# Attention scores through one folded projection, and its neighbours' table subtractions moved

## The reference, cut to what matters

```python
b_ = conv1x1(x, w1, b1).reshape(Bb, Cc, N)
c_ = conv1x1(x, w2, b2).reshape(Bb, Cc, N)
d_ = conv1x1(x, w3, b3).reshape(Bb, Cc, N)
scores = jnp.einsum('bci,bcj->bij', c_, b_)
A = jax.nn.softmax(scores, axis=1)
attn = jnp.einsum('bcj,bkj->bck', d_, A)
```

## Time and profile before

| what | value |
|---|---|
| median of 3 runs | 163.59 us (163.04 to 163.64) |
| profiled execution, its own time | 163.81 us |
| its span, first to last instruction | 162.0 us |
| granted TensorE clock, mean | 0.973 of full speed |
| TensorE busy | 143.1 us (88%) |
| VectorE busy | 114.4 us (71%) |
| ScalarE busy | 87.2 us (54%) |
| GpSimd busy | 57.4 us (35%) |
| attention, S2 to the first convolution | 13.92 to 82.40 us |
| chain that ended last | TensorE 63%, VectorE 19%, issue 8%, ScalarE 5% |

### The profile page before, as it was taken

The page is one execution under the profiler, slowest core; times in us unless marked ns, Lnnn a source line. Parts: engine busy times, 40 slices in busy tenths (PEclk is TensorE's granted clock), DMA queues, the critical chain, the costliest instruction groups (busy, mean ns, idle before and its releaser), DMA issues.

```text
span 162.0 us, 2623 instructions
## 1 busy us (share of the span) xinstructions
PE 143.1 (88%) x948; PEld 65.8 (41%) x951; DVE 114.4 (71%) x270; ACT 87.2 (54%) x141; POOL 57.4 (35%) x109
## 2 busy tenths in 40 slices
PE   7888999999999999999999997999979996899400
PEld 2153422324221242222235763776357622388200
DVE  2186598897699977899860857795782477684891
ACT  3245545666754777558652303996192538422571
POOL 7008999999999904100000000000065000000360
PEclk9999999999999999999999999999999999999955
DMA  3496000000000000000000000001000000000007
GB/s 94 122 280 260 4 0 2 0 2 0 0 4 2 0 0 0 0 4 0 0 0 0 0 2 0 4 0 36 0 0 4 0 0 0 0 4 6 0 12 247
DMA packets 2044, 4.41 MB, mean 27 GB/s; under 512 B 240, under 2 KB 752, under 8 KB 1904
## 3 DMA queue, kind: packets, MB, share of 16 engines
q1 hardware_dynamic: 1888, 4.12, 8.0%
q10 hardware_dynamic: 144, 0.13, 0.3%
HBM read 3.06 MB, written 1.05 MB: 25 GB/s over the span
## 4 chain that ended last, share of the span: by engine, by line
PE 63%; DVE 19%; issue 8%; ACT 5%; DMA 3%; DVEq 0%; ACTq 0%
PE ps L395 13%; PE ps L441 12%; PE ps L384 12%; PE ps L458 6%; PE ps L455 4%; DVE nmax L969 4%; DMA wbc<-wa 3%; PE ps L603 2%; DVE dz L859 2%; DVE box_t L1169 2%; PE ps L358 2%; PE ps L347 2%; PE ps L612 2%; DVE tmpo L1080 1%; PE ps L348 1%
## 5 line engine op out<-in xcount | busy, mean ns | idle before, releaser
L649 ACT ACTIVATE probs<-ps,nmax 128x1024 f32<-128x1024 f32 x32 | 35.6, 1113 | 27.7 <-DVE nmax L969 27.1
L969 DVE TENSOR_REDUCE nmax<-ps 128x1 f32<-128x1024 f32 x32 | 39.1, 1221 | 7.2 <-PE ps L384 7.0
L395 PE MATMUL ps<-probs,dz 128*64 128x512 f32 x128 | 33.4, 616 | 1.0 <-DVE dz L859 0.6
L384 PE MATMUL ps<-c,b 64*128 64x512 f32 x128 | 32.0, 613 | 0.5 <-ACT probs L649 0.5
L1272 POOL TENSOR_SCALAR x<-y,ev_bias 128x512 f32<-128x512 f32 x4 | 4.5, 1136 | 53.6 <-ACT y L649 53.4
L384 PEld LDWEIGHTS ps<-c,b 64*128 64x128 f32 x128 | 11.0, 186 | 18.3 <-issue 9.3
L395 PEld LDWEIGHTS ps<-probs,dz 128*64 128x64 f32 x128 | 6.5, 134 | 25.1 <-DVE dz L859 12.5
L441 PE MATMUL ps<-img,wq 128*128 128x512 f32 x48 | 13.3, 418 | 1.0 <-ACT img L649 0.8
L1234 POOL TENSOR_TENSOR box_t<-parm,consts 128x256 f32<-128x256 f32 x24 | 13.9, 613 | 0.0
L866 DVE TENSOR_TENSOR img<-y,img 128x512 fp32r<-128x512 f32 x11 | 8.2, 743 | 7.2 <-ACT y L649 7.2
L859 DVE TENSOR_SCALAR dz<-d,rz 128x64 f32<-128x64 f32 x32 | 11.9, 373 | 1.1
(11 more groups left out here) (166 smaller groups left out, 222.2 us busy)
## 6 DMA issues: line engine op xcount, KB each, us to landing
wraw<-wconv SPq DMA_DIRECT2D x1, 1152.0 KB, 8.7
xd<-x SPq DMA_DIRECT2D x4, 256.0 KB, 5.4
out<-box_t SPq DMA_DIRECT2D x4, 256.0 KB, 2.8
consts<-cst SPq DMA_DIRECT2D x1, 327.0 KB, 5.4
wdd<-wa SPq DMA_DIRECT2D x1, 192.0 KB, 2.4
parm<-par SPq DMA_DIRECT2D x1, 163.0 KB, 2.5
w3x<-w SPq DMA_DIRECT2D x2, 72.0 KB, 2.0
wbc<-wa ACTq DMA_DIRECT2D x1, 131.0 KB, 4.1
```

The costliest lines, as they stand in the source:

```text
L384: last = mm(o[:, 512 * p:512 * p + 512], b32[across, b % 2, j], c32[across, b % 2, :], start=True, stop=True)
L395: last = mm(y[64 * p:64 * p + 64, :], dz[:, g % 4, :], probs[:, g % 3, 512 * p:512 * p + 512], start=False, stop=t == JT - 1)
L649: return nc.scalar.activation(o, i, f, **kw)
L969: V.tensor_reduce(nmax[:, i:i + 1], slot(("S", i)), AX.X, ALU.min).then_inc(max_ready, 1)
```

## The change

For images 1 to 3, B and C are replaced by one projection G = -(W2^T W1 x_j + W2^T b1), and x itself is the other operand of the scores. The 64x64 product of the two weights and the bias are made once on TensorE after tile 2 and read out by VectorE after tile 3. G1 follows tile 4 of image 0, G2 tile 6 of image 0, G3 tile 5 of image 1. Each is written by ScalarE (`g32`), and SyncE copies it with its halves swapped (`g_other`), since half of the score matmuls need it on the other partitions. The residual of image b stands beside G of image b+1; that of image 3 stands alone after tile 5 of image 2. Image 0 keeps B and C. GpSimd subtracts the columns after all four low parts of attention; VectorE subtracts the rows after the last low part of the third convolution, in four pieces of 512.

```diff
-def c_after(b):
-    return 5
-def b_after(b):
-    return 1 if b == 0 else 0
+G_AFTER = {(0, 4): 1, (0, 6): 2, (1, 5): 3}
+R_LAST = (2, 5)
...
                 uses.append(("D", 0))
-            if b + 1 < NB and t in (b_after(b), c_after(b), D_AFTER):
-                uses.append(({b_after(b): "B", c_after(b): "C", D_AFTER: "D"}[t], b + 1))
+            if b + 1 < NB and t == D_AFTER:
+                uses.append(("D", b + 1))
+            if (b, t) in G_AFTER:
+                uses.append(("G", G_AFTER[b, t]))
     return uses
...
-def build(nc, x, wa, wconv, par, cst, out):
+def build(nc, x, wa, wg_raw, wconv, par, cst, out):
     uses = attention_uses()
...
         xd = sa("xd", [NB, HALF])
-        b32 = sa("b32", [2, HW])
-        c32 = sa("c32", [2, HALF])
+        b32 = sa("b32", [HW])
+        c32 = sa("c32", [HALF])
+        g32 = sa("g32", [NB - 1, HALF])
+        g_other = sa("g_other", [NB - 1, HALF])
+        wg = sa("wgr", [256])
+        wgg = sa("wgg", [C])
+        ng = sa("ng", [1])
         d32 = sa("d32", [2, JT, C])
...
         w_sum, w_fold, w_val, biases = (sem(n) for n in ("w_sum", "w_fold", "w_val", "biases"))
+        wg_in, g_fold, g_ready, g_in = sem("wg_in"), sem("g_fold"), sem("g_ready"), sems("g_in", NB - 1)
         warm_zero, b_first = sem("warm_zero"), sem("b_first")
...
             sp.dma_start(xd[:, 1, :], x[:, HALF:2 * HALF]).then_inc(x_in[1], 16)
+            sp.dma_start(wg[0:64], wg_raw).then_inc(wg_in, 16)
             sp.dma_start(consts[:], cst).then_inc(cst_in, 16)
...
             sp.dma_start(wraw[:].rearrange("q k n -> q (k n)"), wconv).then_inc(wconv_in, 16)
+            for b in range(1, NB):
+                sp.wait_ge(act_step, act_after[("G", b)])
+                for half in range(2):
+                    sp.dma_start(g_other[64 * half:64 * half + 64, b - 1, :],
+                                 g32[64 - 64 * half:128 - 64 * half, b - 1, :]).then_inc(g_in[b - 1], 16)
             sp.wait_ge(wq_ready[3], 4)
...
+            def residual(b, p):
+                if p == 0 and b >= 2:
+                    pe.wait_ge(gen[0], b - 1)
+                q = slice(64 * p, 64 * p + 64)
+                mm(ps[q, 6 + b % 2, :], wds[q, 64 * p:64 * p + 64], xd[q, b, :], start=b >= 1, stop=False)
             def project(n, kind, b):
...
                 if kind == "C":
-                    if b >= 2:
-                        pe.wait_ge(gen[0], b - 1)
                     for p in range(2):
                         q, across = slice(64 * p, 64 * p + 64), slice(64 - 64 * p, 128 - 64 * p)
-                        if b >= 1:
-                            mm(ps[q, 6 + b % 2, :], wds[q, 64 * p:64 * p + 64], xd[q, b, :], start=True, stop=False)
                         last = mm(o[across, 0:HALF], wbc[q, 128 + 64 * p:192 + 64 * p], xd[q, b, :],
                                   start=True, stop=True)
+                    last.then_inc(bc_ready, 1)
+                    return
+                if kind == "G":
+                    pe.wait_ge(g_ready, 2)
+                    for p in range(2):
+                        q, across = slice(64 * p, 64 * p + 64), slice(64 - 64 * p, 128 - 64 * p)
+                        residual(b - 1, p)
+                        last = mm(o[across, 0:HALF], wgg[q, :], xd[q, b, :], start=True, stop=True)
                     last.then_inc(bc_ready, 1)
...
                 elif g > 0 and t == 0:
-                    pe.wait_ge(act_step, act_after[("B", b)])
-                    pe.wait_ge(act_step, act_after[("C", b)])
+                    pe.wait_ge(act_step, act_after[("G", b)])
+                    pe.wait_ge(g_in[b - 1], 32)
                 wait_slot(n)
...
                 for p in range(2):
-                    across = slice(64 - 64 * p, 128 - 64 * p)
-                    last = mm(o[:, 512 * p:512 * p + 512], b32[across, b % 2, j], c32[across, b % 2, :],
-                              start=True, stop=True)
+                    q, across = slice(64 * p, 64 * p + 64), slice(64 - 64 * p, 128 - 64 * p)
+                    if b == 0:
+                        rows, cols = b32[across, j], c32[across, :]
+                    else:
+                        of_j = g_other if t // (JT // 2) == p else g32
+                        first = 128 * (t % (JT // 2))
+                        rows, cols = of_j[q, b - 1, first:first + 128], xd[q, b, :]
+                    last = mm(o[:, 512 * p:512 * p + 512], rows, cols, start=True, stop=True)
                 last.then_inc(s_ready, 1)
...
                 y = ps[:, 6 + b % 2, :]
-                if g == 0:
-                    mm(y, wds[:], xd[:, b, :], start=True, stop=False)
                 pe.wait_ge(dz_ready, g + 1)
...
                     last = mm(y[64 * p:64 * p + 64, :], dz[:, g % 4, :], probs[:, g % 3, 512 * p:512 * p + 512],
-                              start=False, stop=t == JT - 1)
+                              start=g == 0, stop=t == JT - 1)
                 last.then_inc(pv_done, 1)
...
                         mm(ps[:, 7, 64:128], b3b[0:64, :], wds[0:64, 0:64], start=True, stop=True).then_inc(w_fold, 1)
+                    if i == 2:
+                        pe.wait_ge(wg_in, 16)
+                        pe.wait_ge(w_val, 2)
+                        mm(ps[:, 7, 128:192], wg[0:64, 0:128], wg[0:64, 128:192], start=True, stop=True)
+                        mm(ps[:, 7, 192:193], wg[0:64, 128:256], wbc[0:64, 256 + P_B1:257 + P_B1],
+                           start=True, stop=True).then_inc(g_fold, 1)
+                    if divmod(i, JT) == R_LAST:
+                        residual(NB - 1, 0)
+                        residual(NB - 1, 1)
                     if i % 2 and i >= 3:
...
             pe.wait_ge(hblk_ready, 2)
-            pe.wait_ge(rows_ready, PIECES)
+            pe.wait_ge(rows_ready, 4)
             pe.wait_ge(cols_placed, NB)
...
-            def b_out(b):
-                act.wait_ge(bc_ready, 2 * b + 1)
-                run(b32[:, b % 2, :], slot(("B", b)), ACT.Identity, bias=head(P_B1)).then_inc(act_step, 1)
-            def c_out(b):
-                act.wait_ge(bc_ready, 2 * b + 2)
-                run(c32[:, b % 2, :], slot(("C", b))[:, 0:HALF], ACT.Identity, bias=nb2[:], scale=-1.0)\
+            def g_out(b):
+                act.wait_ge(g_ready, 2)
+                act.wait_ge(bc_ready, 2 + b)
+                run(g32[:, b - 1, :], slot(("G", b))[:, 0:HALF], ACT.Identity, bias=ng[:], scale=-1.0)\
                     .then_inc(act_step, 1)
...
             act.wait_ge(bc_ready, 1)
-            run(c32[:, 0, :], slot(("C", 0))[:, 0:HALF], ACT.Identity, bias=nb2[:], scale=-1.0).then_inc(act_step, 1)
+            run(c32[:], slot(("C", 0))[:, 0:HALF], ACT.Identity, bias=nb2[:], scale=-1.0).then_inc(act_step, 1)
             act.wait_ge(bc_ready, 2)
-            run(b32[:, 0, HALF:HW], slot(("B", 0))[:, HALF:HW], ACT.Identity, bias=head(P_B1))\
+            run(b32[:, HALF:HW], slot(("B", 0))[:, HALF:HW], ACT.Identity, bias=head(P_B1))\
                 .then_inc(act_step, 1)
...
                 exponentials(i)
-                if b + 1 < NB:
-                    if t == b_after(b):
-                        b_out(b + 1)
-                    if t == c_after(b):
-                        c_out(b + 1)
+                if (b, t) in G_AFTER:
+                    g_out(G_AFTER[b, t])
                 if t == 3 and b >= 1:
...
                 for cols in (slice(0, 128), slice(128, HALF)):
-                    V.tensor_scalar(b32[:, 0, cols], slot(("B", 0))[:, cols], head(P_B1), None, ALU.add)\
+                    V.tensor_scalar(b32[:, cols], slot(("B", 0))[:, cols], head(P_B1), None, ALU.add)\
                         .then_inc(b_first, 1)
...
                 V.tensor_scalar(wval[:], ps[:, 7, 0:64], alpha, None, ALU.mult).then_inc(w_val, 1)
-                link(V.tensor_scalar(brow[:], ps[:, 7, 64:128], alpha, None, ALU.mult))
+                V.tensor_scalar(brow[:], ps[:, 7, 64:128], alpha, None, ALU.mult).then_inc(w_val, 1)
+            def score_weights():
+                dve.wait_ge(g_fold, 1)
+                V.tensor_copy(wgg[:], ps[:, 7, 128:192]).then_inc(g_ready, 1)
+                V.tensor_scalar(ng[:], ps[:, 7, 192:193], -1.0, None, ALU.mult).then_inc(g_ready, 1)
...
                 dve.wait_ge(d_ready, b + 1)
+                if b == 0:
+                    dve.wait_ge(w_val, 2)
                 if b >= 2:
...
                         low_part(0, b - 1)
+                if i == 3:
+                    score_weights()
                 if i == 5:
...
             low_part(2, 3)
+            dve.wait_ge(edge_clip, 4 * PIECES)
+            for i in range(4):
+                n = slice(512 * i, 512 * i + 512)
+                V.tensor_tensor(edge_buf[0][:, n], edge_buf[0][:, n], edge_buf[1][:, n], ALU.subtract)\
+                    .then_inc(rows_ready, 1)
             dve.wait_ge(img3_zero, 1)
...
```

(14 more changed lines are left out.)

## The result

The changed kernel takes 161.06 us, the median of 6 runs (160.12 to 162.54); the kernel before, run beside it, 163.53 (162.89 to 163.99). The ratio is 0.9852, its 95% interval 0.981 to 0.9893: 2.4 us less, 1.8 to 3.1. Of the six runs the slowest, 162.54 us, is counted as slow and left out of the ratio. Forecast were 162.2 us and faster.

What follows compares the result with a forecast made beforehand. TensorE's queue was taken to bound attention except where it meets VectorE. Attention's -3.1 us and the first convolution's +1.8 gave -1.3 on 163.59, or 162.3, with the tile by tile value a forecast of 162.2 us; range 160.4 to 163.9.

Steps and rivals of the forecast that it cites:

- The start of attention: Image 0 up to image 1's first tile: S2 takes B1's place, G replaces projections; a gain of 1.0 us.
- B2 and its stall: Image 1: removing B2 saves 0.85 us, but 0.65 us comes back as a stall for dz of tile 9.
- the rival that VectorE becomes the bound: Attention: without B2 and B3 more stalls come, the gain halves to 1.5 us, total 163.9; chance 0.14.
- B3 and the relief: Attention: removing B3 in image 2 saves 0.85 us; GpSimd's subtractions leaving attention save another 0.85 us.
- The residual alone: Attention, where C3 becomes a residual pair alone: 0.95 us for 1.02, a gain put at 0.05 us.
- Attention in all: The whole attention stage: 3.1 us less, bounds 2.0 and 3.7.
- The columns in the first convolution: GpSimd's 8 subtractions each hold one VectorE operation by 0.5 us; last statistic 1.8 us late, bounds 0 and 3.35.
- the room of 2.17: First convolution: VectorE's idle time before its last statistic, 2.17 us, which absorbs part of its delay.
- Full blocking: Rival, first convolution: each of GpSimd's eight stops VectorE for its whole 0.69 us, 3.35 us, total 163.8; chance 0.10.
- Rows, transfers, the early residual wait: Third convolution's row subtractions fit a 4.3 us gap, added swaps and image 1's output wait are covered: no cost.
- the rival of hidden columns: First convolution: VectorE loses at most its 2.2 us of room, total 160.5, up to 161.3; chance 0.24.

Runs made afterwards that it cites:

- the moved `lsq_gains`: Changed kernel with lsq_gains (two tiny VectorE operations) after tile 11 instead of tile 9; 160.03 us, ratio 0.9776.
- the tables alone: Kernel before with only the table subtractions moved out of attention (columns later on GpSimd, rows on VectorE), B and C projections kept; 163.47 us, ratio 1.0002.
- the kernel with the three moves: Changed kernel with columns after the inner normalisation, lsq_gains after tile 11, third image buffer cleared at the start; 159.74 us, ratio 0.9754.
- without the ramps: Three moves on the changed kernel, with GpSimd's 64 ramp sums and clips left out and tables zero (output not the reference's); 158.76 us, ratio 0.9694.

## Why the prediction was right, and where it was not

- **The start of attention:** 1.0 us forecast, 0.89 measured at tile 8, step by step as written (S2 in B1's place, the fold in the wait, G and residual in 1.02). Right.
- **B2 and its stall:** 0.85 less 0.65 forecast; tiles 8 to 12 gained 0.23, with a stall of 0.50 at the very place, and the moved `lsq_gains` gave the 0.85 back in one execution, 0.47 in another. Right, and the rival that VectorE becomes the bound is true for these tiles only.
- **B3 and the relief:** 0.85 + 0.85 forecast; tiles 15 to 19 gained 1.71. Both sizes are right, but they hang together in a way that the prediction did not say. The relief pays by itself (0.89 at these tiles with the tables alone), and B3's matmuls, put back into the changed kernel, cost their 0.85. Without the relief B3's removal paid only 0 to 0.2: while GpSimd subtracts, VectorE sets these tiles, and TensorE's free time is filled with waiting.
- **The residual alone:** 0.95 us forecast for 1.02; it is 1.01 in the trace (55.60 to 56.61). A miss of 0.06 (and 1.02 less 0.95 is 0.07, where the prediction wrote 0.05).
- **Attention in all:** 3.1 forecast, 3.24 measured.
- **The columns in the first convolution:** 1.8 us late forecast, 0.62 measured. This is the step that failed, by its size: "each holds up one VectorE operation by 0.5 us", eight times. VectorE's end came 2.74 us later instead of 4.0, and the room of 2.17 was right. Six of the eleven operations were held, not eight: the rounding of the weights by 0.42, the main weights by 0.36, four two-column operations by 0.49 each. The two 64-partition pieces of the weights (0.72 us for both, as in before) and the last two single-column scales (0.15 each) were not, though GpSimd was running. So the price of one was right (0.46 us on average), and the number of them was not.
- **Full blocking:** the Trainium skill, "SBUF — State Buffer", "Who interferes with whom", names the kinds: two inputs in SBUF, or a copy or `tensor_scalar` in a 2-port mode, which its operands must qualify for, block against a GpSimd instruction. I read that rule as a price for whatever VectorE would do, 3.35 us. The trace agrees with it for the products of columns, held at one value per partition, and with full blocking at the four in a row: 0.69 us apart, the whole GpSimd interval. What I left out is that not every `tensor_scalar` qualifies. The rows of the two 64-partition pieces fit that: with 192 columns each takes about 0.35 us beside an idle GpSimd (0.72 for both), what the held operation takes for 384 (0.36), so they run at about half its rate. That this is why they passed, and the same for the scales of one column, is argued from the durations; no run shows it by itself. The durations stood in the trace of the kernel before, but no row of it has such a piece or scale beside a busy GpSimd.
- **Rows, transfers, the early residual wait:** nothing forecast; the stretch from the last statistic to the end is 64.4 against 64.5, each transfer of a swap landed in 2.3 us, no wait for image 1's output shows. Right.

So the forecast of 162.2 was 1.1 us high almost wholly by the one term, 1.8 against 0.62. 161.06 lies outside the forecast's own 161.8 to 162.8 and inside the 160.5 to 161.3 of the rival of hidden columns, which had 0.24. That rival is not what happened either: VectorE lost 2.74 us, more than the room of 2.2 that it allowed, and what the prediction took for evidence of it, dz slipping in between two of GpSimd's operations, is not what saved the time.

## What to carry to other kernels

A queue's slack is spent once: taking work off TensorE pays only at tiles where VectorE is in time, so look, at each removed instruction, at what else had been using the time it took. Two edits that relieve both sides of such a place can be worth more together than alone; in attention 1.35 us (0.42 where the clearing met a dz) and 0.96 us gave 3.24 here. When an engine's work is moved beside another's, do not price that other's operations by their number: look in a trace for each form of them beside the busy engine. And read a term of half a microsecond from more than one execution; the same tiles differed by up to that much between traces of nearly the same kernel.

## What the hardware showed that was not expected

- A GpSimd memset of 2.03 us held a 0.26 us `tensor_scalar` for as long as it ran: 1.64 us, where the same dz met it at 0.44 us in; 0.47 and 0.53 us where it met the tail.
- In one execution, the slowest of its kernel, the granted clock of TensorE read 0.56 over 3.3 us after a stand of 1.90 us, and each score step took twice its time; after stands of 1.05 and 1.20 us in another kernel the clock read 1.00 and the steps kept their 0.43.
- The runs of the kernel with the three moves lie within 1.0 us, without the ramps within 0.3 us; the changed kernel's lie within 2.4. These are four to six runs each. That it is the phase between the two engines is argued from the tiles where the executions part, not shown by itself.
